# Fewer waits in the rank loop, the gathers and the layers of a graph kernel, and the second sort's table made behind the second norm

## The reference

```python
h = relu(layernorm(x))                      # x: 3125 x 64
q, k, v = h @ Wq + bq, h @ Wk + bk, h @ Wv + bv          # 8 heads of 8
logits = (q[dst] * k[src]).sum(-1) * 8 ** -0.5 + edge_attr
x = x + (segment_sum(v[src] * segment_softmax(logits, dst), dst) @ Wo + bo)
h = relu(layernorm(x))
e = h @ W_P_w + W_P_b + W_pos               # 3125 x 128, 4 heads of 32
for l in range(2):                          # rows = src, cols = dst
    a = exp(clip((e @ qT[l])[src] . (e @ kT[l])[dst], -10, 10))
    a = a / (segment_sum(a, src)[src] + 1e-8)
    e = layernorm(segment_sum(a * (e @ vT[l])[dst], src) + e) * scale[l] + bias[l]
x = x + (e @ inv_w + inv_b)
```

## Time and profile before

| | us |
|---|---|
| median of 3 runs | 3119.13 (3114.89 to 3119.57) |
| the profiled execution | 3102.02 |
| its span, first to last instruction | 3100.0 |
| PE busy | 2059.2 (66%) |
| DVE busy | 1759.3 (57%) |
| POOL busy | 1726.4 (56%) |
| ACT busy | 1138.2 (37%) |
| mean granted TensorE clock | 0.652 of full |

### The profile page before, as it was taken

How to read it: one execution, slowest core, us unless ns; L and a number is a source line. 1 busy time by engine, 2 the same in 40 slices (tenths; PEclk the granted TensorE clock), 3 DMA queues, 4 the chain that set the end, 5 groups by cost and what they waited for, 6 DMA issues and landing times.

```text
span 3100.0 us, 40313 instructions
## 1 busy us (share of the span) xinstructions
PE 2059.2 (66%) x10636; PEld 1709.9 (55%) x10636; DVE 1759.3 (57%) x6158; ACT 1138.2 (37%) x3026; POOL 1726.4 (56%) x1755
## 2 busy tenths in 40 slices
PE   6777667764365656660977777776676777677675
PEld 4544444443233333330865777776664777677675
DVE  9766566666377776558983343444446443444344
ACT  8433333331045455550114333333333333333331
POOL 1566666665666666660003666666662666666661
PEclk8555555555577777775987566666767666766665
DMA  2000000002222222230003333333342333333332
GB/s 77 3 4 4 4 4 4 4 4 91 69 66 66 67 66 69 68 54 2 2 1 117 108 111 113 106 113 106 109 103 87 106 112 110 107 109 110 112 98 35
DMA packets 114127, 209.60 MB, mean 68 GB/s; under 512 B 46138, under 2 KB 57212, under 8 KB 113532
## 3 DMA queue, kind: packets, MB, share of 16 engines
q0 software_dynamic: 69632, 146.42, 17.6%
q1 hardware_dynamic: 44284, 60.61, 6.5%
HBM read 193.30 MB, written 13.60 MB: 67 GB/s over the span
## 4 chain that ended last, share of the span: by engine, by line
PE 18%; another core or an unknown queue 15%; DVE 13%; issue 12%; POOL 6%; ACT 1%; DMA 1%; DVEq 0%; POOLq 0%; ACTq 0%
PE PS L1412 6%; PE PS L1422 4%; PE PS L1184 4%; DVE work L1338 3%; POOL kv L927 3%; DVE red L1343 2%; POOL arena L1318 2%; PE PS L1424 2%; DVE work L1355 2%; POOL kv L1318 1%; DVE work L1330 1%; DVE work L739 1%; ACT kv L748 1%; PE PS L1269 1%
## 5 line engine op out<-in xcount | busy, mean ns | idle before, releaser
L1318 POOL DMA_INDIRECT arena<-kv_d,S x528 | 518.2, 981 | 280.4 <-issue 145.3
L1412 PE MATMUL PS<-arena,work 128*128 x1760 | 401.5, 400 | 342.7 <-DVE work L1338 227.4
L1318 POOL DMA_INDIRECT kv<-kv_d,S x352 | 343.9, 977 | 432.6 <-DMA kv_d<-arena 251.7
L665 POOL DMA_INDIRECT sorted_d<-S,rows x416 | 422.6, 1016 | 265.4 <-issue 115.8
L1422 PE MATMUL PS<-work,R 128*128 128x128 f32 x1760 | 551.2, 410 | 20.4 <-issue 12.0
L927 POOL DMA_INDIRECT kv<-kv_d,S x440 | 426.8, 970 | 246.1 <-issue 115.4
L1412 PEld LDWEIGHTS PS<-arena,work 128*128 128x128 f32 x1760 | 347.4, 293 | 356.2 <-issue 355.5
L1379 ACT ACTIVATE R<-iota,gate 128x128 f32<-128x128 f32 x880 | 280.0, 388 | 438.2 <-remote 338.5
L1422 PEld LDWEIGHTS PS<-work,R 128*128 128x128 f32 x1760 | 402.4, 280 | 27.4 <-issue 26.5
L1424 PEld LDWEIGHTS PS<-wts,R 128*128 128x128 f32 x1760 | 395.1, 276 | 14.0 <-issue 13.7
L760 PE MATMUL PS<-kv,work 128*128 128x440 f16 x832 | 232.2, 438 | 208.6 <-DVE work L739 94.7
(11 more groups left out here) (268 smaller groups left out, 3188.2 us busy)
## 6 DMA issues: line engine op xcount, KB each, us to landing
work<-segT_d SPq DMA_DIRECT2D x165, 256.0 KB
kv<-kv_d,S POOLq DMA_INDIRECT x792
arena<-kv_d,S POOLq DMA_INDIRECT x528
sorted_d<-S,rows POOLq DMA_INDIRECT x416
kv_d<-arena SPq DMA_DIRECT2D x12, 512.0 KB, 2.9
sorted_d<-S SPq DMA_DIRECT2D x1, 2200.0 KB, 8.5
S<-sorted_d SPq DMA_DIRECT2D x1, 2040.0 KB, 8.9
work<-in_edge_attr_dram SPq DMA_DIRECT2D x1, 1660.0 KB
```

The lines of the kernel that those rows point to most:

```text
L665: gp.indirect_dma_start(out=sorted_d, out_offset=bass.IndirectOffsetOnAxis(ap=rows0[0:n, c:c + 1], axis=0), in_=S0[0:n, c, :], in_offset=N ...
L1318: gp.indirect_dma_start(out=ring[s][:, j, :], out_offset=None, in_=kv1_d[l], in_offset=bass.IndirectOffsetOnAxis(ap=S1[:, t, 1:2], axis=0) ...
L1412: done = nc.tensor.matmul(banks[7][:, j * DM:(j + 1) * DM], RT[:, g % 2, j * P:(j + 1) * P], table[:, ds(blocks[g % 3][j] * (3 * DM), DM)] ...
```

## The change

Three things are done:

- Waits go that another wait on the same engine covers. In the rank loop: `s_first` before L513 on DVE, `s_ats` before the transposes and `s_diag` before the keys on PE, `s_look` before the table copy on ACT. In stage A: `s_qe0`, `s_red0`, `s_lg0` and every other `s_segb0` on DVE, `s_prod0` on PE, three of four `s_row1` on ACT. In the layers: `s_vw1` on POOL, `s_qe1` and `s_exp1` on DVE, `s_sum1` on ACT but for the last group, `s_RT1` (but for the first group) and `s_R1` on PE. The program has 855 semaphore instructions fewer on PE, 745 on DVE, 520 on ACT and 209 on POOL.
- `turned_vector` leaves group `NG - 3` of stage A and stands behind `norm_vector(dve, 1, ...)`. ACT now copies the two sums out of PSUM at the end of `a_scalar`, and its tensors lie elsewhere (`marks`, `words1`). The clearing of banks 2 and 3 moves into `max_vector`, beside that of bank 4. PE runs the last two turns behind the spreading of the last group.
- In `max_vector` the scans come first, the node lines behind them, and the scan of head 4 waits for the last turn, since its lines lie where the turns' operands lay.

```diff
-                        since(dve, s_first, u - 1)
                         dve.wait_ge(s_bc, u + 1)
...
                 pe.wait_ge(s_oh, NEG + g + 1)
-                since(pe, s_ats, g)
...
-                    pe.wait_ge(s_diag, u + 1)
                     since(pe, s_first, u - 1)
...
-                        since(act, s_look, u)
                         table(u + 2, (u + 1) % 2)
...
         def stairs_scalar(act, m):
-            act.wait_ge(s_row1, m * EG // PC + 1)
+            if m * EG % PC == 0:
+                act.wait_ge(s_row1, m * EG // PC + 1)
...
         def turned_vector(dve):
-            dve.wait_ge(s_turn1, CG)
-            sums, words = turned[0:2], turned[2:4]
+            dve.wait_ge(s_sums1, 2)
+            sums, words = sums1, words1
             word, none, word_n = sums[0], words[0], words[1].bitcast(i32)
-            for n in range(2):
-                done = nc.vector.tensor_copy(sums[n], STAIRS[n])
-            vstep(done)
...
-            for n in range(2):
-                nc.vector.memset(banks[2 + n], 0.0)
             dve.wait_ge(s_S1, 1)
...
                 for m in turned_groups(g):
                     lanes_vector(dve, m)
-                if g == NG - 3:
-                    turned_vector(dve)
...
                 for m in turned_groups(g - 1):
-                    turn_tensor(pe, m)
-            for m in turned_groups(NG - 1):
+                    if m < CG - INV:
+                        turn_tensor(pe, m)
+            for m in range(CG - INV, CG):
                 turn_tensor(pe, m)
...
                     stairs_scalar(act, m)
+            act.wait_ge(s_turn1, CG)
+            for n in range(2):
+                nc.scalar.copy(sums1[n], STAIRS[n]).then_inc(s_sums1, 1)
...
+            for h in range(H0):
+                if h == CLEAR:
+                    dve.wait_ge(s_turn1, CG)
+                forward(h, LGT)
+                backward(h, LGT)
...
-            for h in range(H0):
-                forward(h, LGT)
-                done = backward(h, LGT)
...
             dve.wait_ge(s_lines, 2)
-            nc.vector.memset(banks[4], 0.0).then_inc(s_clear0, 1)
+            dve.wait_ge(s_sums1, 2)
+            for n in (2, 3, 4):
+                done = nc.vector.memset(banks[n], 0.0)
+            done.then_inc(s_clear0, 1)
...
                 s = n % RING
-                since(gp, s_vw1, n - RING + 1)
                 since(gp, s_sum1, n - LEAD)
...
                 act.wait_ge(s_clip1, n + 1)
-                since(act, s_sum1, n - 2)
+                if g + 1 == NG:
+                    since(act, s_sum1, n - 2)
...
-                pe.wait_ge(s_RT1, n + 1)
+                if g == 0:
+                    pe.wait_ge(s_RT1, n + 1)
                 since(pe, s_prod1, n)
...
-                pe.wait_ge(s_R1, n + 1)
                 pe.wait_ge(s_vw1, n + 1)
...
             norm_vector(dve, 1, hs, sq)
+            turned_vector(dve)
```

More of the change, by code:

```diff
@@ L44 @@
 INV = 2
+CLEAR = 4
 FREE = 68
@@ L114, in build @@
         span0 = sb("span0", [1, HI], i32)
-        lane1 = sb("lane1", [P, EC], f16)
-        low1 = sb("low1", [P, EC], f16)
-        high1 = sb("high1", [P, EC], f16)
-        back1 = sb("back1", [P, EC])
+        marks = sb("marks", [P, 3 * EC // 2 + EC])
+        lane1, low1, high1 = (marks[:, n * EC // 2:(n + 1) * EC // 2].bitcast(f16) for n in range(3))
+        back1 = marks[:, 3 * EC // 2:3 * EC // 2 + EC]
+        sums1 = [marks[:, n * T:(n + 1) * T] for n in range(2)]
         S1 = sb("S1", [P, T, 2], i32)
@@ L237, in build @@
         stairs = take(INV, EG, T, dt=f16)
-        take = taker(kv_flat, near)
-        turned = [take(T) for _ in range(4)]
+        take = taker(kv_flat, NPAD)
+        words1 = [take(T) for _ in range(2)]
         fwd = kv_flat[:, 0:(H0 + 1) * (T + 2)].rearrange("p (h t) -> p h t", h=H0 + 1)
@@ L344, in build @@
         s_out = sem("s_out")
+        s_sums1 = sem("s_sums1")
         s_S1 = sem("s_S1")
@@ L966, in one_hot_t @@
                 u = g // (BC // TG)
-                dve.wait_ge(s_segb0[u % 4], 16 * (u // 4 + 1))
-                since(dve, s_qe0, g - 1)
+                if g % (BC // TG) == 0:
+                    dve.wait_ge(s_segb0[u % 4], 16 * (u // 4 + 1))
                 at = (g % (BC // TG)) * TG * P
@@ L980, in a_vector @@
                 dve.wait_ge(s_qe0, g + 1)
-                since(dve, s_red0, g - 1)
                 nc.vector.tensor_tensor(prod[:, g % 2, :, 0:D0], kv_near[:, g % SLOTS, :, 0:D0],
@@ L985, in a_vector @@
                 dve.wait_ge(s_prod0, g + 1)
-                since(dve, s_lg0, g - 1)
                 nc.vector.tensor_reduce(red[:, g % 2, :].rearrange("p (j h) -> p j h", j=TG),
@@ L1012, in a_tensor @@
                 pe.wait_ge(s_RT0, g + 1)
-                since(pe, s_prod0, g - 1)
                 for j in range(TG):
@@ L1055, in max_vector @@
                 nc.vector.memset(line[:, :, 0:1], -BIG)
-                nc.vector.memset(line[:, :, T + 1:T + 2], -BIG)
-            for h in range(H0):
-                forward(h, LGT)
-                done = backward(h, LGT)
+                done = nc.vector.memset(line[:, :, T + 1:T + 2], -BIG)
             vstep(done)
@@ L1327, in one_hot_t @@
                     dve.wait_ge(s_segb1[u % 4], 16 * (u // 4 + 1))
-                since(dve, s_qe1, n - 1)
                 at = (g % (BC // TG)) * TG * P
@@ L1341, in logits @@
                 dve.wait_ge(s_prod1, n + 1)
-                since(dve, s_exp1, n - 1)
                 nc.vector.tensor_reduce(red[:, g % 2, 0:TG * H1].rearrange("p (j h) -> p j h", j=TG),
```

## The result

The changed kernel takes **3072.21 us** (median of 5 runs, 3067.17 to 3082.97), the kernel before beside it 3119.13 (5 runs, 3114.89 to 3122.47). The ratio of the two, taken over their executions, is 0.9871, with a 95% interval from 0.9854 to 0.9889: 1.3% faster, or 40 us. The medians alone lie further apart, 47 us. The sum had said 38.

The account below looks back on a forecast made before the run. POOL's run and pause of indirect DMAs were taken to set the pace, with PE's releases late while POOL issues. 30 + 5 + 3 = 38 us off the median 3119.13 gave 3081 us; own range 3062 to 3096, stated range 3040 to 3130.

Parts of the forecast that it names:

- The bound: In four long stages no engine is full; POOL's run and pause set the pace, so shortening pauses counts in full.
- POOL's second wait: In the layers, s_vw1 costs POOL 0.49 us at a pause; removing it gains 30 us, range 0 to 40.
- the upper bound: In the layers, 82 pauses times 0.49 us for POOL's removed wait: 40 us.
- The second estimate: In the layers, early groups' pace of 1.479 us per gather against 1.500, over 880 gathers: 19 us.
- The end of stage A: DVE's table leaves the last group's path: maximum 6 us earlier, clearings return 1.02; gain 5 us, ends 4 and 8.5.
- The table behind the norm: Behind the second norm, the table's 4.8 us fit into DVE's 5.78 us idle gap: cost zero.
- The early waits: Removed waits in the rank loop and stage A: 3 us, from zero to bounds of 33 and 9 us.
- The layers' other waits: Removed waits in the layers other than POOL's: nothing, with a bound of 18 us for PE's s_prod1.
- Rival 1: Layers: PE is as slow as its releases say, POOL's earlier restart brings nothing; gain 6 us, 3113 us, chance 0.26.
- Rival 2: Rank loop, stage A and layers: every removed wait was on the path; gain 105 us, 3014 us, chance 0.08.
- Rival 3: Layers: POOL runs by 8 in place of 12, with pauses of 3.54 us, 35 us slower; 3146 us, chance 0.14.
- What was to show it: POOL restarting 0.23 us behind ACT, 12 gathers in 17.5 us, DVE's norm gap about 1 us, rank loop at 1.53.

Follow-up runs that it names:

- POOL silent: Changed kernel with each of POOL's indirect DMAs in the layers replaced by a plain DMA of the same size issued by SP: 2391.84 us, ratio 0.7679.
- the table alone: Changed kernel with all removed waits put back in the rank loop, stage A and the layers: 3114.42 us, ratio 0.9993.
- the limit of six: Changed kernel with LEAD 6 in place of 4, so POOL may be six groups ahead of the sums: 3090.54 us, ratio 0.9897.
- the two that ran by 16: Changed kernel with POOL's s_vw1 wait put back, 3059.03 us; kernel before without the layers' other removed waits, POOL's two kept, 3072.48 us.
- runs of no less than 12: Changed kernel with POOL waiting for s_sum1 at every third group only: 2737.06 us, ratio 1.0003.

## Why the prediction was right

3081 was forecast and 3072 measured, with the range and the sign right. The gain was 38 in the sum, 40 by the ratio, and 47 by the medians. By its steps:

- **The bound.** "POOL's run and pause set the pace, and what shortens the pause counts in full" was told as a reading. It holds: POOL silent takes 721 us off the kernel before, and PE, with its number of matmuls unchanged, runs a layer in half the time, at the higher clock. A swap of two lines that only moves POOL's restart brings the whole gain of the removed wait. It holds only where the releases are late: in the fastest condition there was nothing to shorten.
- **POOL's second wait, 30 us (0 to 40).** 27 was measured by itself, and 16 where the kernel before took 3078; the layers' stage marks gave 27 and 29 for all their removed waits together. The price of a wait was right, 0.48 for 0.49. The way there was not: the upper bound multiplied it by the 82 pauses of runs of 12, and those runs are gone. That 30 came out so near is in part luck, since it is the middle between this bound and 19. The second estimate, the pace of the early groups, 1.479 per gather, had the better mechanism: the changed kernel runs all groups as the early ones ran, by eight, at 11.87 us for 8, 1.484 here and 1.474 over the layer. It had given 19 us because the 18.00 us for 12 that it was held against, 1.500, was a good stretch; over the two layers the kernel before took 1.502 and 1.509, from which the same step gives 23.
- **The end of stage A, 5 us.** The two pairs show 4.5 and 5.7 up to stage B, the table alone 4.8. The gather of the last group is what is late next, as said, and the last turns delay nothing. The two clearings and the node lines come back in the maximum.
- **The table behind the norm, 0.** 8.51 us before and 8.36 after.
- **The early waits, 3 us.** 5, with zero at the edge of the interval. The rule of the Trainium skill, "VectorE: DVE Perf Modes", section "The DRAIN you can't avoid", which would give 0, can't be told from it here. **The layers' other waits, nothing:** 5 us, with 0 outside the interval, so this term was undersized. No row tells which of the removed waits had been met when they were reached, so these 5 us neither bear that rule out nor refute it. These two errors and the 3 us too many for POOL cancel in part, and that is luck too.
- **Rival 1** falls with POOL silent. **Rival 2**, 105 us, falls with the four parts measured one by one. **Rival 3** was half right, and the more instructive half: POOL does run by 8 now. Its price was wrong. It took the old pause less the second wait, 3.54, for the new one, and set the point that decides at 3.25. The pause became 2.95. It was not a fixed piece but grew with the run before it: in the kernel before it was 3.96 us in the mean behind 12 gathers (60 times) and 3.06 behind 8 (9 times), in the changed one 2.93 behind 8 (102 times) and 4.4 behind 20, and 5.7 behind 28 with the limit of six. Of the 1.03 us between 3.96 and 2.93 the wait can be 0.48. (Its 35 us are also rounded up: with 1.536 in place of 1.54 the same sum is 32.) The early groups' 2.82, which stood beside it, was the row to believe.
- **What was to show it:** the restart 0.24 us behind ACT came, the 17.5 us for 12 gathers did not, the gap behind the norm came to 0.88, and the rank loop stayed at 1.52.

## What to carry to other kernels

If an instruction has two waits, look in the trace which of them ends last, and write that one first: the one written second became an instruction of its own here and cost POOL 0.48 us at each restart, while a removed wait and a swapped one were worth the same. If several stages with quite different work all share one rate, find the engine whose run and pause make it, and price a change by pauses; expect the pattern of the runs to change with them, and take the pace of a stretch that already runs in the new way over the old number of pauses times a saving. Before giving credit to such a change, time both kernels on several chips and more than once: here it was worth 40 us, and in another condition, under a chip number where the kernel before had been slow minutes earlier, a kernel that contains it gained nothing.

## What the runs showed of the hardware

- From a release to the start it took 0.259 us for POOL's indirect DMA with one wait, and 0.74 with the wait in an instruction of its own in front (46 of 76 pauses, and the median). This isn't one price for all kernels: in the two that ran by 16 the median was 0.49, and only 12 of 58 and 17 of 57 pauses took 0.74. Why is open.
- PE's releases came late only where POOL issues indirect DMAs: in the kernel before none of the 173 from 3 us behind POOL's last gather of stage A to its first of the layers, and two thirds by over 0.5 us in the layers. In the changed kernel those that end a pause come 2.7 us behind the start of POOL's last DMA (the median of 105), and in 104 of these cases one more comes 0.6 to 1.4 us into the next run.
- That isn't a fixed property. The same kernel before took 3119, 3078, 3113, 3122 and 2736 us in the five comparisons, the last two under one chip number, and in the trace taken beside the last, of the kernel with runs of no less than 12, no release was late. What makes the difference wasn't found, and no experiment here reaches it. It is worth some 380 us, against 40 of the change.
- In the changed kernel 90 of the 880 indirect DMAs of the layers kept POOL for over 1 us, 1.14 on average, where most take 0.95; without POOL's wait alone it was 99 at 1.30. The other removed waits by themselves don't shorten them: with those gone and POOL's two kept it was 161 at 1.28. The cause wasn't tried.
